# A perceiver block on one core: TensorE's turn in a new order, with the output projection a turn later

## What is computed

```
x = x + xattn(layernorm(x), ctx)      # 16 heads of 8, causal and key mask, softmax, out @ Wo
x = x + attn(layernorm(x))            # 16 heads; q = x@Wq; latent = (x@Wk + x@Wv) @ W_down
                                      # k = latent@W_up_k, v = latent@W_up_v
                                      # scores = clip(q.k * scale, +-1e4) * decay(|i-j|)
                                      # softmax(scores) @ v, then @ Wo
x = x + ffn(layernorm(x))             # two linear layers, x, h and weights rounded to 8-bit
                                      # steps by one scale per tensor, exact gelu between
```

## Time and profile before

| | |
|---|---|
| median of 3 runs | 336.77 us (335.54 to 338.06) |
| the profiled execution's own time | 335.31 us |
| its span, first to last instruction | 333.4 us |
| mean granted clock of PE | 0.964 of full speed |
| PE busy | 295.4 us (89%) |
| DVE busy | 261.1 us (78%) |
| ACT busy | 255.0 us (76%) |
| POOL busy | 231.9 us (70%) |

### The profile page before, as it was taken

One profiled execution on the slowest core, in us unless ns is written; L12 is line 12 of the kernel. 1 busy time (PEld: TensorE's weight loads), 2 busy tenths in 40 slices (PEclk: granted clock), 3 DMA queues, 4 the chain that ended last, 5 costly groups with the idle time before them and its releaser, 6 DMA issues.

```text
span 333.4 us, 13004 instructions
## 1 busy us (share of the span) xinstructions
PE 295.4 (89%) x5391; PEld 201.9 (61%) x5392; DVE 261.1 (78%) x563; ACT 255.0 (76%) x554; POOL 231.9 (70%) x166
## 2 busy tenths in 40 slices
PE   4796979999999999999999998999999987375785
PEld 2454758676776677676757575656667675221264
DVE  1496768989787888887878876868788996679876
ACT  3487867686769887888787879798869758499592
POOL 5187758767688886699999998978999960063000
PEclk9899999999999999999999999999999999769679
DMA  8998000000000000000000000000000000000026
GB/s 193 239 195 167 3 2 4 2 2 3 5 3 2 4 2 6 2 4 2 2 2 6 2 2 2 4 4 3 4 2 2 4 4 2 2 0 0 0 65 189
DMA packets 19099, 9.49 MB, mean 28 GB/s; under 512 B 5153, under 2 KB 18786, under 8 KB 19042
## 3 DMA queue, kind: packets, MB, share of 16 engines
q1 hardware_dynamic: 18322, 8.25, 11.7%
q10 hardware_dynamic: 720, 0.43, 0.6%
HBM read 6.57 MB, written 2.10 MB: 26 GB/s over the span
## 4 chain that ended last, share of the span: by engine, by line
PE 68%; ACT 18%; DVE 6%; issue 6%; DMA 1%; SPq 0%; DVEq 0%; ACTq 0%
PE ps L549 11%; PE ps L567 9%; PE ps L525 9%; PE ps L573 7%; PE ps L583 7%; PE ps L458 4%; ACT arena L841 4%; PE ps L449 4%; ACT vx L728 3%; PE ps L465 3%; PE ps L546 3%; ACT pt L762 2%; ACT xn3T L674 2%; PE ps L431 2%; PE ps L629 2%
## 5 line engine op out<-in xcount | busy, mean ns | idle before, releaser
L762 ACT ACTIVATE pt<-ps 128x512 f32<-128x512 f32 x128 | 75.8, 594 | 23.9 <-PE ps L549 23.8
L376 POOL TENSOR_TENSOR u<-u,mx 128x1024 f32<-128x1024 f32 x32 | 60.9, 1904 | 37.8 <-DVE mx L972 37.7
L368 POOL TENSOR_TENSOR ud<-u,con 128x1024 f32<-128x1024 f32 x31 | 73.4, 2369 | 4.0 <-DVE u L958 3.9
L953 DVE SCALAR_TENSOR_TENSOR u<-ps,rs,arena 128x1024 f32<-128x1024 f32 x32 | 41.0, 1283 | 18.8 <-PE ps L525 18.7
L958 DVE TENSOR_SCALAR u<-ps 128x1024 f32<-128x1024 f32 x32 | 39.1, 1223 | 16.4 <-PE ps L525 13.7
L525 PE MATMUL ps<-arena,qT 32*64 32x256 f32 x1024 | 44.0, 400 | 6.4 <-ACT arena L755 4.3
L567 PEld LDWEIGHTS ps<-pt,vx 128*32 128x32 f32 x2048 | 31.7, 109 | 26.0 <-issue 15.9
L376 POOL TENSOR_TENSOR ud<-ud,mx 128x768 f32<-128x768 f32 x30 | 44.2, 1474 | 2.4
L567 PE MATMUL ps<-pt,vx 128*32 128x64 f32 x2048 | 41.9, 222 | 1.9 <-ACT pt L762 1.1
L755 ACT ACTIVATE arena<-kT,cst,con 128x512 f32<-128x512 f32 x51 | 41.6, 820 | 0.3
L573 PE MATMUL ps<-pt,con 128*32 128x128 f32 x1024 | 39.8, 273 | 0.0
(11 more groups left out here) (148 smaller groups left out, 548.9 us busy)
## 6 DMA issues: line engine op xcount, KB each, us to landing
out<-pt SPq DMA_DIRECT2D x8, 256.0 KB, 2.3
x<-in_x SPq DMA_DIRECT2D x4, 256.0 KB, 4.0
arena<-in_ctx SPq DMA_DIRECT2D x8, 128.0 KB, 4.2
x<-in_x SPq DMA_DIRECT2D x2, 512.0 KB, 7.8
arena<-in_ctx SPq DMA_DIRECT2D x4, 256.0 KB, 6.8
arena<-in_mask_BxS_if SPq DMA_DIRECT2D x2, 256.0 KB, 5.7
arena<-in_mask_BxS_if SPq DMA_DIRECT2D x4, 64.0 KB, 4.0
arena<-in_mask_BxS_if SPq DMA_DIRECT2D x2, 128.0 KB, 3.8
```

Source lines behind the costliest of these rows:

```text
L368: pool.tensor_tensor(dh, uh, decay.unsqueeze(1).to_broadcast([P, H, HALF]), ALU.mult)\
L376: pool.tensor_tensor(uh, uh, mx[:, n % 4, 0:count].unsqueeze(2).to_broadcast([P, count, HALF]), ALU.subtract)\
L762: act.activation(pt[:, n % 2, 4 * half:4 * half + 4].rearrange("p h n -> p (h n)"), ps[:, bank, :], ACT.Exp).then_inc(s["emptied"], 1)
L953: dve.scalar_tensor_tensor(by_head(u[:, n % UB]), sc, rs[:, 0, n:n + 1], mask[:, n].unsqueeze(1).to_broadcast([P, H, HALF]), ALU.mult, ALU ...
```

## The change

PE's turn gets a new order: scores(n), project(n - 5), the pieces, the transposes of tile n - 2, the maxima's products (a function of its own, `shift_keys`), values(n - 3) and sums. From turn 64 on the pieces come last. The projection comes five turns behind the scores in place of four (LAG_ADD), and the division four in place of three (LAG_DIV). The maxima's products are 8 of 32 columns in place of 4 of 64. The ring of banks follows the new order. ACT makes the logarithm and reciprocal first, then the pieces, then both exponents; DVE divides right behind `add_residual` and ahead of the maxima. The turns at which the last norm's steps are due move by one.

```diff
--- before.py
+++ after.py
@@ -40,10 +40,10 @@
 ON_POOL = (0, 1)
 BATCH = (((0, 4), (4, 4), (8, 4), (12, 4), (16, 8), (24, 8)), tuple((4 * g, 4) for g in range(8)),
          ((0, 8), (8, 8), (16, 8), (24, 4), (28, 4)))
-ROOT_TURN = ((-1, 1, 4, 7, 12, 17), tuple(17 + 4 * g for g in range(8)), (45, 53, 61, 65, 68))
+ROOT_TURN = ((-1, 1, 4, 7, 12, 17), tuple(17 + 4 * g for g in range(8)), (46, 54, 62, 66, 69))
 POOLED = 4
 APPLY_TURN = tuple(21 + 4 * g for g in range(POOLED, 8))
-APPLY3 = (49, 51, 57, 59, 63, 64, 66, 69)
+APPLY3 = (50, 52, 58, 60, 64, 65, 67, 70)
 BY_ACT = 6
 ON_PE = 4
 HS = H - ON_PE
@@ -55,7 +55,7 @@
 CHUNK = (0, 1, 2, 3, 4, 4, 5, 5)
 MASKS = ((0, 4), (4, 8), (8, 16), (16, 32))
 MAKE = ((-1, 0, 4, 0), (0, 4, 8, 1), (2, 8, 16, 2), (5, 16, 24, 3), (8, 24, 32, 3))
-LAG_T, LAG_PV, LAG_ADD = 2, 3, 4
+LAG_T, LAG_PV, LAG_DIV, LAG_ADD = 2, 3, 4, 5
 
 EPS = 1e-5
 CLAMP = 10000.0
@@ -107,8 +107,7 @@
     for turn in pieces:
         project = [("o", turn - LAG_ADD)] if 0 <= turn - LAG_ADD < NS else []
         to_keys = [("t", turn - LAG_T, half) for half in range(2)] if 0 <= turn - LAG_T < NS else []
-        order += to_keys + project if turn > NS else project + to_keys
-        order += pieces[turn]
+        order += project + (pieces[turn] + to_keys if turn < NS else to_keys + pieces[turn])
     by_act = [what for what in order if what[0] != "o"]
     return pieces, order, {what: n for n, what in enumerate(by_act)}
 
@@ -535,23 +534,27 @@
                 elif half == 0:
                     pe.wait_ge(s["shifted_dve"], n - (NS - BY_DVE) + 1)
                 bank = bank_of(("t", n, half))
-                if n == NT:
-                    pe.wait_ge(s["ident_cast"], 2)
-                if layer == 1 and half == 1:
-                    pe.wait_ge(s["maxed16"], t + 1)
-                on_pe = [h for h in range(4 * P // HALF) if layer == 1 and half == 1 and h + H // 2 >= HS]
                 for i in range(HP // 2):
                     hp = half * 4 + i
-                    if on_pe:
-                        last = pe.matmul(ps[:, bank, i * P:(i + 1) * P], src[:, hp * P:(hp + 1) * P], ident,
-                                         is_transpose=True, start=(i == 0), stop=False)
+                    out_t, in_t = ps[:, bank, i * P:(i + 1) * P], src[:, hp * P:(hp + 1) * P]
+                    if layer == 1 and half == 1:
+                        last = pe.matmul(out_t, in_t, ident, is_transpose=True, start=(i == 0), stop=False)
                     else:
-                        last = pe.transpose(ps[:, bank, i * P:(i + 1) * P], src[:, hp * P:(hp + 1) * P], ident)
-                for h in on_pe:
-                    e, i = h % 2, h // 2
-                    last = pe.matmul(ps[HALF * e:HALF * (e + 1), bank, i * P:(i + 1) * P],
-                                     mx16[:, n % 4, h + H // 2 - HS:h + H // 2 - HS + 1].to_broadcast([P, HALF]),
-                                     minus_i[:, :], start=False, stop=(h in on_pe[-2:]))
+                        last = pe.transpose(out_t, in_t, ident)
+                if layer == 0 or half == 0:
+                    last.then_inc(s["filled"], 1)
+
+            def shift_keys(n):
+
+                layer, t = layer_of(n)
+                pe.wait_ge(s["maxed16"], t + 1)
+                bank = RB + slot["t", n, 1] % NR
+                for h in range(HS, H):
+                    i, e = divmod(h - H // 2, 2)
+                    for r in (2 * e, 2 * e + 1):
+                        last = pe.matmul(ps[32 * r:32 * (r + 1), bank, i * P:(i + 1) * P],
+                                         mx16[:, n % 4, h - HS:h - HS + 1].to_broadcast([P, 32]), minus_i[:, :],
+                                         start=False, stop=(h >= H - 2))
                 last.then_inc(s["filled"], 1)
 
             def values(n):
@@ -589,17 +592,20 @@
             for n in TURNS:
                 if n < NS:
                     scores(n)
-                if n == NS + 1:
+                if 0 <= n - LAG_ADD < NS:
+                    project(n - LAG_ADD)
+                for what in pieces[n] if n < NS else ():
+                    piece(what)
+                if 0 <= n - LAG_T < NS:
                     to_keys(n - LAG_T, 0)
                     to_keys(n - LAG_T, 1)
+                if n - LAG_T == NT:
+                    pe.wait_ge(s["ident_cast"], 2)
+                if NT <= n - LAG_T < NS:
+                    shift_keys(n - LAG_T)
                 if 0 <= n - LAG_PV < NS:
                     values(n - LAG_PV)
-                if 0 <= n - LAG_ADD < NS:
-                    project(n - LAG_ADD)
-                if LAG_T <= n <= NS:
-                    to_keys(n - LAG_T, 0)
-                    to_keys(n - LAG_T, 1)
-                for what in pieces[n]:
+                for what in pieces[n] if n >= NS else ():
                     piece(what)
 
             pe.wait_ge(s["emptied"], max(fill.values()) + 1)
@@ -797,18 +803,16 @@
                     expand(0, 0)
             root(0, 0)
             for n in TURNS:
-                there, den = 0 <= n - LAG_T < NS, 0 <= n - LAG_PV < NS
-                if there and n > NS:
+                if 0 <= n - LAG_DIV < NS:
+                    log_den(n - LAG_DIV)
+                    inv_den(n - LAG_DIV)
+                for what in pieces[n] if n < NS else ():
+                    piece(what)
+                if 0 <= n - LAG_T < NS:
                     exponent(n - LAG_T, 0)
                     exponent(n - LAG_T, 1)
-                if den:
-                    log_den(n - LAG_PV)
-                if there and n <= NS:
-                    exponent(n - LAG_T, 0)
-                if den:
-                    inv_den(n - LAG_PV)
-                if there and n <= NS:
-                    exponent(n - LAG_T, 1)
+                for what in pieces[n] if n >= NS else ():
+                    piece(what)
                 for k in range(3):
                     for m, turn in enumerate(ROOT_TURN[k]):
                         if turn == n:
@@ -820,8 +824,6 @@
                 for g, turn in enumerate(APPLY3):
                     if g < BY_ACT and turn <= n <= turn + 1:
                         normalise3(g, n - turn)
-                for what in pieces[n]:
-                    piece(what)
                 for j in range(1, 2 * NG):
                     for h in range(HR):
                         if RING3 <= j < NG and h in ON_POOL:
@@ -959,6 +961,8 @@
                         .then_inc(s["clipped"], 1)
                 if 0 <= n - LAG_ADD < NS:
                     add_residual(n - LAG_ADD)
+                if 0 <= n - LAG_DIV < NS:
+                    divide(n - LAG_DIV)
                 if n < NS:
                     dve.wait_ge(s["s_read"] if n < NT else s["clipped"], n + 1 if n < NT else t + 1)
                     if layer:
@@ -971,8 +975,6 @@
                     else:
                         dve.tensor_reduce(mx[:, n % 4], by_head(u[:, n % UB]), AX.X, ALU.max)\
                             .then_inc(s["maxed"], 1)
-                if 0 <= n - LAG_PV < NS:
-                    divide(n - LAG_PV)
                 if n == NS - 1:
                     shift_last(n - 1)
                     decay_last(n)
```

## The result

| | before | after |
|---|---|---|
| median of 4 runs | 337.06 us (335.54 to 338.06) | 354.82 us (353.81 to 359.41) |
| ratio, 95% interval | | 1.052 (1.047 to 1.058) |
| the profiled execution: time, span | 335.31, 333.4 us | 354.51, 352.6 us |

A forecast was written before the change was run, and what follows sets the result against it. PE was taken to bound most turns, with POOL keeping equal pace in late layer 1. Terms 1.1 + 13.9 + 3.9 = +18.9 us on 335.3 gave 354.2, by the median 355.7, given as 355; range 345 to 364.

The forecast's parts named there:

- The ring of banks (step 2): PE's second half of the transposes waits for the same turn's projection bank until DVE's residual, standing 0.3 to 0.75 us.
- The sign asked for: On PE's timeline, a gap ahead of the second half put down to DVE's residual, in nearly all turns from 4 to 55.
- 2.16 us up to the residual: Scores' start to DVE's residual, in both layers; with 0.41 to PE, the second half can't start before 2.57 us.
- The forecast for turns 9 to 34: Layer 0, turns 9 to 33: 111.5 us against 97.65 before, loss 13.9 us; a turn with one piece takes 4.17.
- For turns 34 to 56: Layer 1, turns 34 to 55: 98.9 us against 95.0 before, loss 3.9 us; a turn with one piece takes 4.30.
- Turns with v and c: The second half waits for ACT's four copies of v: 5.25 us a turn, 5.8 with a third piece.
- with two pieces: The first half waits for the projection's bank until 2.57 us and the second starts 0.46 later: 4.63 us a turn.
- Turns 4 to 9: Turns 4 to 8 lose 2.8 us by counting, partly hidden by waits for expanded keys: 1.1 taken, bounds 0 and 2.8.
- The switches (step 1): Fewer changes of matmul shape on PE: work of a layer-1 turn with a piece falls by 0.24 us or a little more.
- ACT's lateness in layer 1: In four turns normalisation delays logarithm, reciprocal, division and values instead of v's copies: 0.85 us each, 3.4 in all.
- POOL's 3.88 us: POOL's time for each tile in late layer 1, said to set the pace from turn 56 on: no gain, no loss.
- the chain behind the last scores: Sums, logarithm, reciprocal, division, values and projection of the last tiles, said to be as before: 0, bounds 0 and 0.5 us.

The follow-up runs named there:

- the spare instruction: DVE multiplication of 128x128 constants that nobody reads, ahead of each add_residual: on the changed kernel 365.73 us (1.086), on the kernel before 347.79 us (1.032).

## Why the prediction was right, and where it was off

**The ring of banks (step 2)** was right as the cause. The row ahead of the second half names DVE's residual, plain turns all have the same length whatever their piece, and work put between read and residual lengthens them one to one. The sign asked for "in nearly all turns" is only partly seen in the rows: between 40 and 255 us the list of waits names the residual 14 times, since with k, q or v the gap is 0.2 us or less. There the equal lengths and the spare instruction show the loop. With the residual and division ahead of the read, plain turns of layer 0 return to 3.79 us, while the later projection alone costs nothing.

**Its size was a little off.** I took 2.16 us up to the residual from the earlier trace rows as set by the read. The rows fit the projection better: this starts 1.64 us into the turn, and the residual 0.52 after it. The read alone lets the residual start at 2.10 in layer 0 (104.13 less 102.03), and the wait from there to PE is 0.34, not 0.41. That gives 2.44 in place of 2.57, and with the 1.60 for the rest of the turn 4.04 us in place of 4.17. In layer 1 the read lets it start earlier still, in turn 40 after scores at 186.48 (DVE, PE):

```profile
188.49 0.28 DVE L895 TENSOR_TENSOR x<-ps,x 128x128 f32<-128x128 f32 x1
...
188.82 0.66 PE L541 MATMUL ps<-con,ud 128*128 128x128 f32 x4 [0.37 <-DVE x L895]
```

The second half starts 2.34 us into the turn, and the rest takes 1.70: again 4.04, where 4.30 was forecast. That both layers come to 4.04 is chance. The forecast for turns 9 to 34 was 2.5 us too long, nearly all from the plain turns. For turns 34 to 56 the shorter loop takes off 5.7 us; ACT's late turns and those with x3 cost 1.4 more than forecast, which leaves the 4.3.

**Turns with v and c** were forecast at 5.25 and 5.8, and took 5.20 and 5.81; with two pieces 4.63, and 4.54 were taken. Turns 4 to 9 came out at the 1.1 us given; since that was picked between 0 and 2.8, the agreement is in part luck.

**The switches (step 1)** are worth about what the rows said. The 64-column form in the new place costs 0.14 to 0.15 us (0.11 was expected). With the bank and the division out of the way (both calls ahead of the read), turns with x in layer 1 take 3.45 us in place of 3.75: PE's own work fell by 0.30, where 0.24 or a little more was forecast. In layer 0 turn 20 stays at 3.37. The Trainium skill, TensorEngine Tiling (Array Packing), Key Properties, has TensorE drain at each change of tiling mode; these numbers agree with that. By themselves the switches are a gain; in layer 1 the loop took more than was saved in the turns with x (3.75 before, 4.04 after), and left 0.2 us in those with k, q or v.

**ACT's lateness in layer 1** moved as forecast, from v's bank to the reciprocal and the values: 1.24 us over a plain turn in turn 38 (0.85 forecast), 1.23 in 42 and 46, 0.8 in 50. ACT, DVE and PE in turn 38 after:

```profile
178.10 1.64 ACT L680 ACTIVATE xn3T<-x,nmr,rs 128x128 f32<-128x128 f32 x4
...
180.64 0.31 ACT L779 ACTIVATE rden<-lden 128x128 f32<-128x128 f32 x1
...
180.98 0.29 DVE L901 TENSOR_TENSOR oT<-ps,rden 128x128 f32<-128x128 f32 x1 [1.52 <-ACT rden L779]
...
181.42 0.65 PE L570 MATMUL ps<-pt,vx 128*32 128x64 f32 x32 [1.02 <-ACT kT L723]
```

PE's row names ACT's copy of k, which merely ended last by the profile. The values start 0.44 us after the division, as elsewhere, and the division waited for the reciprocal.

**Two terms put at nothing weren't.** From turn 56 on I let POOL's 3.88 us rule. POOL kept that pace in both kernels but wasn't on the chain in either. In turns without a piece the division's loop sets 3.66 us (3.16 before), and those with x3 keep 4.03: 1.6 us. And the chain behind the last scores, which I took to be as before (0, bounds 0 and 0.5), grew by 5.9 us in the profiled execution. It has the same links, but the division moved behind ACT's last norm. At least 2.1 us of this is the order; how much of the other 3.8 is the clock is open. These errors, 7.5 us, cancelled with 6.8 us of turns forecast too long. That the sum came so close is luck; that the loss fell in the range is not, since turns 9 to 34, where the loop was rightly found, carry 11.4 of the 19.2 us.

## What to carry to other kernels

In a ring of buffers a new order of work also decides whose release each entry waits for: write out, entry by entry, which one stood there before, and when in the same turn it is let go. Before a step is moved earlier, look at what its old place covered; a loop through another engine (here scores, read, residual, bank) sets the turn from then on, and when it is opened the next one takes over (here at 3.99 us in place of 4.04). Here ACT, late by a burst of work, stayed late when the burst's parts were reordered; spreading the burst took the wait away (1.1% faster). And look at what a probe does before its result is read: the spare instruction took 0.22 us in most turns and up to 1.66 beside POOL.

## What the runs showed of the hardware

The maxima's products as 4 of 128x64 between groups of 128x128 and 128x32 cost 0.14 to 0.15 us a turn more than as 8 of 128x32. DVE's next instruction starts before the one ahead of it is shown as ended: in turn 20 the residual starts 1.20 us after a read that is shown as 1.28 us long. DVE's multiplication of 128x128 float32 numbers from SBUF to SBUF, 0.22 us long at the median, took 0.78 to 1.66 us in nine turns in which POOL was at work, and ended 0.08 to 0.09 us after an instruction of POOL. With the 64-column products, turn 8 has a stretch with a granted clock of 0.53, near the lower level (1.2 of 2.4 GHz): the 32 matmuls of the values took 1.08 us there (at 51.74), and 0.65 in the changed kernel at 1.00. In the 2.5 us ahead of it PE was busy for 1.65 us in both kernels, and the clock fell in one of them only.
